# A decoder's last cross attention: scores in two halves, exponentials and copies in turn

## The reference

```
q = (queries @ Wq).reshape(b, s, 8, 4, 16)
k = (keys @ Wk).reshape(b, s, 8, 16)
v = (values @ Wv).reshape(b, s, 8, 16)
scores = einsum('bqhgd,bkhd->bhgqk', q, k) * 16 ** -0.5
attn = softmax(scores, axis=-1)
out = einsum('bhgqk,bkhd->bqhgd', attn, v).reshape(b, s, 512) @ Wo
```

## Time and profile before

| | us |
|---|---|
| three runs, median | 2476.78 |
| lowest, highest | 2475.41, 2477.81 |
| the profiled execution | 2474.88 |
| its span in the trace | 2473.0 |
| PE busy | 2365.8 (96%) |
| DVE busy | 1256.6 (51%) |
| ACT busy | 902.7 (37%) |
| POOL busy | 668.7 (27%) |

### The profile page before, as it was taken

One profiled execution on the slowest core, in us unless ns is written; L12 is line 12 of the kernel. 1 busy time (PEld: TensorE's weight loads), 2 busy tenths in 40 slices (PEclk: granted clock), 3 DMA queues, 4 the chain that ended last, 5 costly groups with the idle time before them and its releaser, 6 DMA issues.

```text
span 2473.0 us, 38446 instructions
## 1 busy us (share of the span) xinstructions
PE 2365.8 (96%) x13227; PEld 2020.4 (82%) x13227; DVE 1256.6 (51%) x2917; ACT 902.7 (37%) x2230; POOL 668.7 (27%) x383
## 2 busy tenths in 40 slices
PE   4999899999999999998999999999999999997877
PEld 3788788888888889887888888888888888885555
DVE  6444644445444444456644444444444444457775
ACT  1111344444444444433233333333333333334673
POOL 4334522322222322231311111111111111112541
PEclk9999999999999999999999999999999999998888
DMA  3110312111111211110111111111111111100000
GB/s 117 60 51 26 103 52 75 61 51 61 58 51 63 73 51 51 68 60 27 49 41 45 45 45 45 45 45 45 45 45 45 45 45 45 45 18 0 1 1 34
DMA packets 36830, 118.95 MB, mean 48 GB/s; under 512 B 4904, under 2 KB 7336, under 8 KB 36784
## 3 DMA queue, kind: packets, MB, share of 16 engines
q1 hardware_dynamic: 36784, 118.35, 14.1%
HBM read 116.24 MB, written 2.10 MB: 48 GB/s over the span
## 4 chain that ended last, share of the span: by engine, by line
PE 88%; DVE 5%; issue 3%; POOL 2%; ACT 2%; SPq 0%; DMA 0%; POOLq 0%; ACTq 0%; DVEq 0%
PE pj L542 19%; PE pj L543 18%; PE pj L544 18%; PE ou L542 7%; PE ou L544 6%; PE ou L543 6%; PE pv L720 2%; PE sc L857 2%; PE pv L866 2%; PE sc L704 2%; PE tp L711 1%; POOL w_lo L410 1%; PE sc L967 1%; POOL w_hi L408 1%; ACT probs L1308 1%
## 5 line engine op out<-in xcount | busy, mean ns | idle before, releaser
L402 POOL TENSOR_TENSOR w_lo<-raw,w_hi 128x1024 fp32r<-128x1024 f32 x145 | 346.7, 2392 | 1437.3 <-ACT w_hi L1093 1397.1
L542 PE MATMUL pj<-xt_hi,w_hi 128*128 128x512 f32 x1232 | 498.5, 405 | 5.9 <-POOL w_lo L410 2.3
L543 PE MATMUL pj<-xt_lo,w_hi 128*128 128x512 f32 x1232 | 481.9, 391 | 0.0
L544 PE MATMUL pj<-xt_hi,w_lo 128*128 128x512 f32 x1232 | 481.4, 391 | 0.0
L542 PE MATMUL ou<-w_hi,act_hi 128*128 128x512 f32 x684 | 275.3, 402 | 1.2 <-DVE x L1382 0.6
L542 PEld LDWEIGHTS pj<-xt_hi,w_hi 128*128 128x128 f32 x1232 | 232.8, 189 | 50.2 <-issue 3.1
L544 PEld LDWEIGHTS pj<-xt_hi,w_lo 128*128 128x128 f32 x1232 | 231.8, 188 | 49.5
L544 PE MATMUL ou<-w_hi,act_lo 128*128 128x512 f32 x684 | 267.4, 391 | 0.0
L543 PE MATMUL ou<-w_lo,act_hi 128*128 128x512 f32 x684 | 267.2, 391 | 0.0
L543 PEld LDWEIGHTS pj<-xt_lo,w_hi 128*128 128x128 f32 x1232 | 232.8, 189 | 40.7
L1382 DVE TENSOR_TENSOR x<-x,ou 128x512 f32<-128x512 f32 x192 | 130.9, 685 | 258.1 <-PE ou L544 257.6
(11 more groups left out here) (241 smaller groups left out, 4554.7 us busy)
## 6 DMA issues: line engine op xcount, KB each, us to landing
raw<-in_l1a_w SPq DMA_DIRECT2D x80, 512.0 KB, 4.1
raw<-in_l0x_w SPq DMA_DIRECT2D x64, 512.0 KB, 4.2
side<-in_side SPq DMA_DIRECT2D x32, 512.0 KB, 4.1
raw<-in_ffn_w SPq DMA_DIRECT2D x15, 512.0 KB, 3.4
raw<-in_l0f_w SPq DMA_DIRECT2D x6, 512.0 KB, 3.8
raw<-in_l1x_w SPq DMA_DIRECT2D x6, 512.0 KB, 3.4
raw<-in_taylor_w SPq DMA_DIRECT2D x5, 512.0 KB, 7.1
x<-in_x SPq DMA_DIRECT2D x2, 1024.0 KB, 6.6
```

The costliest lines, as they stand in the source:

```text
L402: pool.tensor_tensor(WL[:, s, :], RAW[:, s, :], f32(WH[:, s, :]), ALU.subtract).then_inc(w_ready[s], 1)
L542: pe.matmul(out, wh, xh, start=first, stop=False)
L543: pe.matmul(out, wh, xl, start=False, stop=False)
L544: return pe.matmul(out, wl, xh, start=False, stop=last)
```

## The change

TensorE computes a group's scores in two halves: parts 0 and 1, which wait for the exponentials 0 and 1 of the group before, and parts 2 and 3, which wait for its exponentials 2 and 3. Half 0 of group n+1 stands ahead of the transposes of parts 0 and 1 of group n, half 1 ahead of those of parts 2 and 3. ACT alternates exponentials of group n+1 with copies of group n, part by part. DVE computes maxima 0 and 1 of group n+1, then the sums 2 and 3 of group n, then maxima 2 and 3, then sums 0 and 1 of group n+1. The heads of a batch come in the turn after, between the second and third pair of steps, for even n from 2 on; the output stays where it was in TensorE's order.

```diff
--- before.py
+++ after.py
@@ -951,17 +951,18 @@
                     last = mm3(bank[:], w, wide(XT, hf)(k), k == 0, k == KC - 1)
                 last.then_inc(q_full, 1)
 
-            def scores(n):
+            def scores(n, two):
 
                 b, part = n // 2, n % 2
-                pe.wait_ge(kx_ready, n + 1)
-                pe.wait_ge(q_out, b // HB * KC + 2 * part + 2)
+                if two == 0:
+                    pe.wait_ge(kx_ready, n + 1)
+                    pe.wait_ge(q_out, b // HB * KC + 2 * part + 2)
                 if n:
-                    pe.wait_ge(lx_exp, n * KG)
-                else:
+                    pe.wait_ge(lx_exp, (n - 1) * KG + 2 * two + 2)
+                elif two:
                     pe.wait_ge(pj_done, PJ["ln4"] + B)
                 for h in range(2):
-                    for g in range(KG):
+                    for g in (2 * two, 2 * two + 1):
                         r = slice(32 * g, 32 * g + 32)
                         at = (2 * part + h) * HALF + b % HB * S
                         last = pe.matmul(score_banks[g][:, h * 256:(h + 1) * 256], AF[r, at:at + S], KX[r, n % 2, :],
@@ -1027,14 +1028,15 @@
             queries(0, 1)
             turn(4, range(6, B))
             queries(0, 2)
-            scores(0)
+            scores(0, 0)
+            scores(0, 1)
             queries(0, 3)
             for n in range(NG):
-                transposes(n, 0)
-                if n + 1 < NG:
-                    scores(n + 1)
-                for g in range(1, KG):
-                    transposes(n, g)
+                for two in range(2):
+                    if n + 1 < NG:
+                        scores(n + 1, two)
+                    transposes(n, 2 * two)
+                    transposes(n, 2 * two + 1)
                 if n % 2 == 0 and n:
                     output(n // 2 - 1)
                 values(n)
@@ -1333,18 +1335,18 @@
             for g in range(1, KG):
                 exps(0, g)
             for n in range(NG - 1):
+                exps(n + 1, 0)
                 turned_out(n, 0)
+                exps(n + 1, 1)
                 turned_out(n, 1)
                 if n == 6:
                     queries(1, 0)
-                exps(n + 1, 0)
+                if n % 2 == 0 and n:
+                    heads(n // 2 - 1)
+                exps(n + 1, 2)
                 turned_out(n, 2)
-                exps(n + 1, 1)
+                exps(n + 1, 3)
                 turned_out(n, 3)
-                exps(n + 1, 2)
-                if n % 2:
-                    heads(n // 2)
-                exps(n + 1, 3)
                 if n == 6:
                     queries(1, 1)
                 if n == 7:
@@ -1917,21 +1919,25 @@
                 row_max(0, g)
             dve.wait_ge(w_hi[3], SLOT["l1x_o"] + 1)
             dve.tensor_tensor(WL[:, 3, :], RAW[:, 3, :], f32(WH[:, 3, :]), ALU.subtract).then_inc(w_ready[3], 1)
-            for g in range(KG):
-                row_sums(0, g)
+            row_sums(0, 0)
+            row_sums(0, 1)
             for n in range(NG - 1):
-                for g in range(KG):
-                    row_max(n + 1, g)
+                row_max(n + 1, 0)
+                row_max(n + 1, 1)
+                row_sums(n, 2)
+                row_sums(n, 3)
+                row_max(n + 1, 2)
+                if n % 2 == 0 and n:
+                    heads(n // 2 - 1)
+                row_max(n + 1, 3)
                 if n in (0, 1):
                     dequantise(2 + n)
                 row_sums(n + 1, 0)
                 row_sums(n + 1, 1)
                 if n % 2 == 0 and n:
                     add(n // 2 - 1)
-                row_sums(n + 1, 2)
-                if n % 2:
-                    heads(n // 2)
-                row_sums(n + 1, 3)
+            row_sums(NG - 1, 2)
+            row_sums(NG - 1, 3)
             heads(B - 1)
 
             def weights_lo(c):
```

## The result

The changed kernel takes 2520.57 us (median of four runs, 2517.61 to 2520.90), the kernel before 2476.82 (four runs, 2475.41 to 2477.81). The ratio is 1.0175, with a 95% interval from 1.0163 to 1.0188. The forecast was slower, 2507, range 2488 to 2521: the side is right, the size is 14 us short.

What follows compares the result with a forecast made beforehand. No engine is full in the edited stage; its turns are a loop of hand-offs. Terms 11.3, 8.0, 9.6, 1.2 and 0.6 sum to 30.7 us on 2474.88, giving 2505.6, put at 2507 as median; range 2488 to 2521.

Steps and rivals of the forecast that it cites:

- The mechanism: ACT ends each turn with copy 3, then idles through values, half the scores and a maximum: about 2.9 us per turn.
- Half a set costs as much as a whole one: TensorE's half scores: 1.15 us each, like the whole set, at 2.4 GHz; bounds 0.58 and 1.15.
- Odd turns: Five plain odd turns at 2.4 GHz: 9.35 us each against a mean of 7.10, +11.3 us in all.
- Queries: Turns 6, 7 and 8, with queries behind values: 15.3, 13.1 and 17.65 us, +9.6 us in all.
- Even turns: Five plain even turns: 10.2 us at 2.4 GHz, 12.1 with the clock's fall, +8.0 us in all.
- Case A: Rival: clock stays at 2.4 GHz in even turns, +20, 2497 us; with short halves +12, 2489, chance 0.20.
- Case B: Rival: clock is low in odd turns too, +44, 2521 us; chance 0.12.
- Turn 1: Turn 1, low clock but a fast values(0): 10.6 us against 9.40, +1.2 us.
- The start: Turn 0, no values ahead, pays only for the second half of the scores: +0.6 us, bounds 0 and 2.
- After values(15): Turn 15 has no scores and keeps the old order; it and what comes after: 0.

Runs made afterwards that it cites:

- e3: Changed kernel with the orders of ACT and DVE undone, TensorE's half scores kept: 2477.68 us, ratio 1.0007 to the kernel before.
- e2: Changed kernel with TensorE's order and whole score sets as before, ACT and DVE as changed: 2533.9 us, ratio 1.0237 to the kernel before.
- e4: Changed kernel with half 0 of scores(n+2) ahead of values(n) and the output, except groups 8 and 9: 2504.12 us, ratio 1.0115.
- e7: Changed kernel with half 0 and transpose (n+1, 0) ahead of values(n) and output, except groups 8 and 9, batch add moved later: 2493.57 us, ratio 1.0074.
- e8: Changed kernel with 8 spare matmuls ahead of values and 4 ahead of transpose 2, in turn 0 and odd turns 1 to 13: 2505.67 us.
- e10: Changed kernel with e8's spare matmuls, the 4 ahead of transpose 2 now in every turn from 0 to 14: 2497.71 us, ratio 1.0103.
- e5: Kernel before the change, with 8 spare matmuls ahead of values in the odd turns 1 to 13: 2467.66 us, ratio 0.9964.

## Why the prediction was right, and where its size was off

- **The mechanism.** Copy 3 as the last thing of ACT's turn, with values, half 0 and a maximum between it and ACT's next piece: shown, by e3 (ACT's and DVE's order undone, no loss left), e2 (TensorE's undone, loss greater), e4 (half 0 taken out of the path, odd turns shorter by just what exponentials 0 came earlier) and e7 (the path taken away, odd turns 6.67). e3 undid ACT and DVE together; which of the two orders carries how much was not separated.
- **Half a set costs as much as a whole one.** Right: 1.13 us against 1.15. That the loss could be the halves themselves is ruled out by e3.
- **Odd turns**, +11.3: right, +11.3, step by step.
- **Queries.** Turns 6 and 7 right (15.18 and 13.10 for 15.3 and 13.1). Turn 8 took 20.34, not 17.65: its values and first queries ran at the low clock, which I had left out, and its scores started 11.08 us after values, not 8.45; in e8 and e10, at 1.00, it took 17.68. The start taken over for turn 6 (5.99) held a stretch of low clock already (its values before ran 1.68 us), that for turn 8 did not.
- **Even turns**, +8.0: the term that was mis-sized; they brought +15.6. The step as put was "I take the same fall: values +0.87, half 0 +0.93, and 0.1 for half 1", 12.1 in all. The fall came, but its length was wrong. I let it end with half 1, so that "output to values takes 2.93". It lasted through both halves, the transposes of all four parts and two thirds of the output. In turn 14 the output started 9.5 us after values (forecast 9.2) and took 4.5 from its start to the next values (2459.16 to 2463.65) for the 2.93. TensorE was busy for all 14 us and set the turn alone, while the sum had gone by the chain of ACT's steps, the heads and the output at full clock. e10 shows the rest of the sum right: at 1.00 the turn is 10.25, forecast 10.2. Of the clock before, the forecast read "0.64 to 0.69 in most even ones"; four of the five had 0.68 or 0.69, turn 14 had 0.84, and 0.64 is turn 1.
- **Case A** (clock up in even turns, +20) is close to e10, once the gaps were filled: from values(0) to values(15) it is 20.6 us over the kernel before. That e10's time of 2497.7 also meets the 2497 is luck: its own kernel before took 2472.2, so it is 25 us slower than that. Left alone, the clock went the other way. Case B's time (2521) was reached, but by another road than it named: the odd turns stayed at 0.91 to 0.99, and the even ones got worse.
- **Turn 1**, +1.2 forecast, +2.8 measured: again the low clock, 0.50 over all of it; e8 has 9.39 us there. **The start**, +0.6 forecast, +1.5 measured, can't be told from the spread between executions: in e5, whose program is that of the kernel before up to values(0), values(0) came 2.5 us later than there.
- **After values(15)**, 0 forecast, +2.3 measured: no run isolates it. values(15) ran at the low clock in the changed kernel, 1.93 us, and at the full one before, 1.07. In the four traces of this case where it ran 1.06 or 1.07 us, the stretch from its start to the end took 46.9 to 47.4 us, in the eight where it ran 1.49 to 1.94 it took 48.2 to 50.8. So the 2.3 us go with the low clock there.

## What to carry to other kernels

When engines hand work round in a loop, look at what each engine still has to do while the slowest hand-off runs. Alternating two kinds of work removed a wait of 27.6 us, but it put the piece that everybody waits for at the very end of ACT's turn, and the next turn's first piece behind it in another queue. And where TensorE pauses for one or two microseconds in such a loop, as here for 1.2 to 2.4, price also the case that the whole turn after it runs at the lower level of the clock, as work of TensorE, and not only as longer steps on somebody else's path.

## What the runs showed of the hardware

- Leaving TensorE idle cost more, through its clock, than matmuls in the idle stretches. Spare matmuls whose results nobody reads took 22.9 us off the changed kernel (2520.57 to 2497.71; these are different sets, and by the ratios to the kernel before it is some 18) and 8.9 off the kernel before (2476.53 to 2467.66, in one).
- The lower level (1.2 GHz) lasted while TensorE was busy without a break: from 2449.66 to 2462.3 in turn 14 of the changed kernel, over values, half sets, transposes and two thirds of the output's 12 matmuls.
- No one length of gap goes with the fall. At the end of every odd turn of the changed kernel values came after a gap of 2.3 to 2.4 us and ran 1.93 or 1.94 us. In the kernel before, values(7) came after a gap of 2.31 us and ran 1.07, and turn 8 had 1.00. In e3, with a gap of 1.77 us, turn 10 had the low clock and turns 4, 12 and 14 had not; its turn 2 came after a turn that was at 0.50 throughout. In e8 the clock fell right after a gap of 1.22 us in turn 14 and stayed at 1.00 over turn 10, with a gap of 1.21 us at the same place. Which of two alike gaps is followed by the fall stays open.
